# Two matmul bursts of a recurrent group in halves, with the last level's sums between, on one Trainium2 core

## The reference, cut to what matters

```python
def step(s, rkvw):
    r_t, k_t, v_t, w_t = rkvw
    a = k_t[..., :, None] * v_t[..., None, :]
    out = jnp.einsum('bhi,bhij->bhj', r_t, u * a + s)
    s = a + w_t[..., :, None] * s
    return (s, out)
...
_, out = jax.lax.scan(step, s0, rkvw)
```

## Time and profile before

| what | value |
|---|---|
| median of 3 runs | 4139.7 us (4137.18 to 4140.56) |
| the profiled execution, its own time | 4149.18 us |
| its span, first to last instruction | 4147.4 us |
| PE busy | 3717.0 us, 90% |
| VectorE, ScalarE, GpSimd busy | 63%, 52%, 40% |
| mean granted TensorE clock | 0.954 |

### The profile page before, as it was taken

How to read it: one execution, slowest core, us unless ns; L and a number is a source line. 1 busy time by engine, 2 the same in 40 slices (tenths; PEclk the granted TensorE clock), 3 DMA queues, 4 the chain that set the end, 5 groups by cost and what they waited for, 6 DMA issues and landing times. The chain is left out here.

```text
span 4147.4 us, 66284 instructions
## 1 busy us (share of the span) xinstructions
PE 3717.0 (90%) x24448; PEld 2274.3 (55%) x24448; DVE 2623.6 (63%) x5691; ACT 2149.6 (52%) x4272; POOL 1650.5 (40%) x1849
## 2 busy tenths in 40 slices
PE   7988899898898889999988888998998889899898
PEld 4544575645554457464655445656465454565556
DVE  4765736766676573676667657467666765646766
ACT  5755743433675574343466657334347575733434
POOL 3554443222455445322245444422325544542232
PEclk9999999999998999999999999999999999999999
DMA  4032220202303222020320412211022032221102
GB/s 137 17 95 71 82 81 26 77 11 78 110 16 96 70 82 81 22 81 11 110 77 15 120 54 83 72 40 63 22 102 80 29 106 56 77 71 42 61 25 109
DMA packets 94528, 275.81 MB, mean 67 GB/s; under 512 B 25472, under 2 KB 25984, under 8 KB 73088
## 3 DMA queue, kind: packets, MB, share of 16 engines
q1 hardware_dynamic: 94208, 271.58, 20.4%
HBM read 201.24 MB, written 4.19 MB: 50 GB/s over the span
## 5 line engine op out<-in xcount | busy, mean ns | idle before, releaser
L813 POOL TENSOR_SCALAR probs<-probs,row_inv 128x512 f32<-128x512 f32 x1024 | 693.0, 692 | 643.6 <-DVE row_inv L728 643.5
L672 ACT ACTIVATE probs<-probs,row_max 128x512 f32<-128x512 f32 x1024 | 733.6, 726 | 129.4 <-DVE row_max L744 128.3
L567 PE MATMUL ps<-ident,probs 128*128 128x128 f32 x4096 | 608.9, 290 | 173.4 <-ACT pT L666 147.2
L567 PEld LDWEIGHTS ps<-ident,probs 128*128 128x128 f32 x4096 | 478.8, 147 | 383.7 <-ACT pT L666 210.7
L666 ACT ACTIVATE pT<-ps 128x512 f32<-128x512 f32 x768 | 430.5, 602 | 113.0 <-PE ps L567 112.3
L377 PE MATMUL ps<-mix,wring 128*128 128x512 f32 x1024 | 477.5, 603 | 5.0 <-DMA wring<-in_blocks_dram 3.4
L542 PE MATMUL ps<-kstack,qstack 96*128 96x512 f32 (+1 forms) x1024 | 380.2, 466 | 19.0 <-DVE row_max L744 10.4
L744 DVE CUSTOM_DVE_ANT_0 probs<-ps,maskA 128x512 f32<-128x512 f32 x512 | 329.3, 681 | 43.9 <-PE ps L542 43.9
L744 DVE CUSTOM_DVE_ANT_0 probs<-ps,neg 128x512 f32<-128x512 f32 x512 | 340.6, 685 | 8.8
L377 PEld LDWEIGHTS ps<-mix,wring 128*128 128x128 f32 x1024 | 193.9, 192 | 204.2 <-issue 184.8
L1543 POOL TENSOR_TENSOR hinv<-hvar,minus_half 128x32 f32<-128x32 f32 x24 | 146.2, 6093 | 378.8 <-DVE hvar L1263 378.8
(11 more groups left out here) (178 smaller groups left out, 7022.5 us busy)
## 6 DMA issues: line engine op xcount, KB each, us to landing
wring<-in_blocks_dram SPq DMA_DIRECT2D x151, 1024.0 KB, 5.2
qstack<-hi SPq DMA_DIRECT2D x256, 64.0 KB, 2.0
kstack<-hi SPq DMA_DIRECT2D x256, 64.0 KB, 2.0
maskA<-in_mask_dram SPq DMA_DIRECT2D x9, 1024.0 KB, 7.6
rows<-in_rows_dram SPq DMA_DIRECT2D x8, 1024.0 KB, 5.9
qstack<-hi SPq DMA_DIRECT2D x256, 32.0 KB, 2.0
qstack<-lo SPq DMA_DIRECT2D x128, 64.0 KB, 2.0
kstack<-lo SPq DMA_DIRECT2D x128, 64.0 KB, 2.0
```

Of the source, the lines that this page charges most:

```text
L567: ins = nc.tensor.transpose(tile[:, qc * P:(qc + 1) * P], probs[:, m % PSLOTS, qc, kc * P:(kc + 1) * P], ident[:, :])
L672: nc.scalar.activation(p, p, ACT.Exp, bias=row_max[:, n % PSLOTS, qc:qc + 1], scale=-1.0, accum_out=row_sum[:, n % PSLOTS, qc:qc + 1]).the ...
L813: nc.gpsimd.tensor_scalar(p, p, row_inv[:, (n - 1) % PSLOTS, qc:qc + 1], 1.0, ALU.mult, ALU.mult)\
```

## The change

In the recurrent groups:

- `fresh_state` and `from_state` take a list of token tiles. Each burst is run as two halves, tiles (0, 1) and (2, 3). The semaphore updates stay at the last tile, the waits at the first.
- `pair_sums4` takes a part. Part 0 stands between the halves of `fresh_state`, part 1 behind them.
- `bonus_high` takes a part. Part 0 stands ahead of `from_state`, part 1 between its halves.
- On VectorE `bonus` level 4 becomes `bonus4(hg, part)`. Part 0 stays where it was; part 1 moves behind `states` and `spread`. `states` is divided into `new_states` (line 1233's joins) and `states` (the scans), with nothing between them.

```diff
-            def pair_sums4(hg):
+            def pair_sums4(hg, part):
                 pe.wait_ge(*dve_done.when('rk', l, hg, 4))
-                for part in range(2):
-                    nc.tensor.matmul(take(pe, 'sums4', l, hg, part), head_sum[:, :], rk4[:, 2 * part:2 * part + 2, :, :],
-                                     start=True, stop=True).then_inc(*tile_ready.reach('sums4', l, hg, part))
+                nc.tensor.matmul(take(pe, 'sums4', l, hg, part), head_sum[:, :], rk4[:, 2 * part:2 * part + 2, :, :],
+                                 start=True, stop=True).then_inc(*tile_ready.reach('sums4', l, hg, part))
...
-            def bonus_high(hg):
+            def bonus_high(hg, part):
                 by8 = y_bank.rearrange('p (b two t) -> p b two t', two=2, t=4)
-                for s in range(4):
-                    if s % 2 == 0:
-                        pe.wait_ge(*dve_emptied.when('sums4', l, hg, s // 2))
+                pe.wait_ge(*dve_emptied.when('sums4', l, hg, part))
+                for s in (2 * part, 2 * part + 1):
                     m = nc.tensor.matmul(by8[:, :, 1, :], centre[:, :], rk4[:, s, :, :], start=False, stop=False,
                                          skip_group_check=True)
-                m.then_inc(*S['context_ready'].reach('high', l, hg))
+                m.then_inc(*S['context_ready'].reach('high', l, hg, part))
...
-                fresh_state(hg)
-                pair_sums4(hg)
+                fresh_state(hg, (0, 1))
+                pair_sums4(hg, 0)
+                fresh_state(hg, (2, 3))
+                pair_sums4(hg, 1)
                 bonus_low(hg)
                 middle(hg, 1)
                 if hg == C - 1:
                     gate(C - 1)
                 if hg > 0:
                     roots_to_features(hg - 1)
-                bonus_high(hg)
-                from_state(hg)
+                bonus_high(hg, 0)
+                from_state(hg, (0, 1))
+                bonus_high(hg, 1)
+                from_state(hg, (2, 3))
                 middle(hg, 2)
...
                 if hg > 0:
-                    dve.wait_ge(*S['context_ready'].when('high', l, hg - 1))
+                    dve.wait_ge(*S['context_ready'].when('high', l, hg - 1, 1))
...
-                bonus(hg, 4)
+                bonus4(hg, 0)
+                new_states(hg)
                 states(hg)
                 spread(hg)
+                bonus4(hg, 1)
                 if hg > 0:
                     normalise(hg - 1)
```

More of the change, by code:

```diff
@@ L962, in keys_to_tokens, with fresh_state @@
                 m.then_inc(*tile_ready.reach('kt', l, hg))
[L964 to L969, removed]
+            def fresh_state(hg, tiles):
+                if 0 in tiles:
+                    for level in range(3):
+                        pe.wait_ge(*dve_emptied.when('sums', l, hg, level))
+                    pe.wait_ge(*act_emptied.when('vt', l, hg))
+                    pe.wait_ge(*act_emptied.when('kt', l, hg))
+                for tc in tiles:
                     for r in range(4):
@@ L976, in fresh_state, with from_state @@
                                                  start=True, stop=True)
[L977 to L986, removed]
+                if C - 1 in tiles:
+                    m.then_inc(*S['fresh_ready'].reach(l, hg))
+            def from_state(hg, tiles):
+                if 0 in tiles:
+                    pe.wait_ge(*dve_done.when('r8', l, hg))
+                    pe.wait_ge(*dve_done.when('fresh', l, hg))
+                    pe.wait_ge(*act_done.when('other', l, hg))
+                    pe.wait_ge(*act_done.when('pairs', l, hg))
+                    pe.wait_ge(*dve_done.when('pairs', l, hg))
+                for tc in tiles:
                     for p in range(4):
@@ L1209, in bonus @@
                 dve.wait_ge(*act_emptied.when('vp', l, hg))
[L1210 to L1227, removed]
@@ L1229, in states @@
-            def states(hg):
+                dve.wait_ge(*tile_ready.when('sums', l, hg, level))
+                if level == 0:
+                    out, i0, i1 = rk0[:, :], ps[:, 0, :], v
+                elif level == 1:
+                    out, i0, i1 = rk1[:, :], ps[:, 1, 0:256], tokens(v, 1)[:, :, 0, 0]
+                else:
+                    out, i0 = rk2[:, :, :, :], ps[:, 2, :].rearrange('p (s b t) -> p s b t', s=2, t=2)
+                    i1 = tokens(v, 2)[:, :, 0, :].rearrange('p b s -> p s b').unsqueeze(3).to_broadcast([P, 2, L // 4, 2])
@@ new lines, in bonus @@
+                nc.vector.tensor_tensor(out, i0, i1, ALU.mult).then_inc(*dve_emptied.reach('sums', l, hg, level))
+            def bonus4(hg, part):
+                dve.wait_ge(*tile_ready.when('sums4', l, hg, part))
+                two = slice(2 * part, 2 * part + 2)
+                i0 = ps[:, ring.bank('sums4', l, hg, part), :].rearrange('p (s b t) -> p s b t', s=2, t=4)
+                i1 = tokens(vT[:, hg % 2, :], 4)[:, :, 0, two].rearrange('p b s -> p s b').unsqueeze(3)\
+                    .to_broadcast([P, 2, L // 8, 4])
+                nc.vector.tensor_tensor(rk4[:, two, :, :], i0, i1, ALU.mult)\
+                    .then_inc(*dve_emptied.reach('sums4', l, hg, part))
@@ L1230, in states, with new_states @@
+            def new_states(hg):
                 dve.wait_ge(*act_done.when('other', l, hg))
@@ L1236, in states @@
                 ins.then_inc(*dve_done.reach('fresh', l, hg))
+            def states(hg):
                 dve.wait_ge(*dve_done.when('fresh', l, hg))
```

3 lines of the change are left out of this document (2 added, 1 removed).

## The result

The changed kernel takes 4167.12 us (median of 6 runs, 4160.81 to 4174.76) against 4136.43 us for the kernel before on the same chip (6 runs, 4122.88 to 4140.56): a ratio of 1.0073, 95% interval 1.0056 to 1.0089. It is slower by 30.7 us. The forecast was +7.4 us; the range to 4170 us held the time, but the likeliest bin, no measurable difference, was wrong.

The account below looks back on a forecast made before the run. PE's own instruction list plus its waits was taken to bound each group. 21.6 us (ordinary groups) + 9.8 (last groups) - 24 (relief) = +7.4 us, the profiled execution going from 4149.2 to 4156.6, median 4147; range 4132 to 4170.

Parts of the forecast that it names:

- likeliest bin: Whole kernel: time within about 0.2% (8.3 us) of the kernel before; chance 0.43.
- The halves: Split bursts on PE: each half takes 0.95 us to the next line; splitting `fresh_state` costs PE 0.28 us.
- The state chain: From `fresh_state` to `from_state`: joins start at about 4.21 us, `pairs` comes 0.24 us earlier, `from_state` can start at 11.38.
- The structure: Added time in the recurrent groups: 21.6 us over 24 ordinary groups plus 9.8 us over 8 last groups.
- The relief: Gaps and low clock around the bursts: 24 us of some 39 go away; bounds 0 and 39.
- more than nine: Test in the new profile: more than nine stretched halves would show the prediction wrong.
- under 8 us of "issue" waits: Test in the new profile: PE's "issue" waits at the bursts fall from about 15 us to under 8.
- forecast gap: PE's stop in a stretched burst: a gap of 2.1 us, start to start, shrinks to 0.9 to 1.
- No relief: Rival on the bursts' gaps and low clock: none of it goes; +31 us, up to +40, 4171 to 4180; chance 0.2.
- Full relief: Rival on the bursts: no gaps or low clock remain; -8 to -12 us, 4128 to 4132; chance 0.15.
- switches cost nothing: Rival on PE's weight-load switches: they hide under running matmuls; 22 us, with relief -2 (4138); chance 0.1.
- the change does nothing: Rival at `from_state`: the wait still covers part 1 of `bonus_high`; within 3 us of 4140; chance 0.07.

Follow-up runs that it names:

- e10: Changed kernel with `spread` (ScalarE's half of `pairs`) moved ahead of the copy of rT on ScalarE; 4159.29 us, ratio 1.0044 to the kernel before.
- e4_again: The kernel before, unchanged, profiled once more; 4119.88 us in one run.
- e6: Kernel before with one token tile of `fresh_state` issued twice in one early group, 64 more PE records; 4135.80 us, ratio 0.9978.
- e7: Kernel before with two token tiles of `fresh_state` issued twice in one early group, 128 more PE records; 4151.05 us, ratio 1.0025.
- e8: Kernel before with three token tiles of `fresh_state` issued twice in one early group, 192 more PE records; 4136.96 us, ratio 0.9990.
- e11: Kernel before with `spread` (ScalarE's half of `pairs`) moved ahead of the copy of rT on ScalarE; 4136.90 us, ratio 1.0004.
- e9: Changed kernel with 128 more PE records issued once in its first group; 4180.73 us, ratio 1.0094 to the kernel before.
- e1: Kernel before with only `fresh_state` in halves, `from_state` whole and VectorE's order as before; 4138.80 us, ratio 0.9998.
- e5: Changed kernel with `from_state` whole, behind both parts of `bonus_high`; 4151.95 us, ratio 1.0032 to the kernel before.
- e2: Kernel before with only `from_state` in halves, part 1 of `bonus_high` between, `fresh_state` whole; 4178.66 us, ratio 1.0099.
- e3: Kernel before with only VectorE's order changed, part 1 of `bonus4` behind `spread`, both bursts whole; 4144.64 us, ratio 1.0020.

## Why the prediction was wrong in size

**Right in kind.** PE's list is what bounds a group; part 1 of `bonus_high` leaves a wait that hid it; PE idles about 0.6 us ahead of `from_state` (0.62); no ring bank and no VectorE part makes PE wait in the changed kernel; gaps shrink rather than grow. The sums between the halves take 1.06 us (688.82 to 689.88) and those behind them 0.97 (690.87 to 691.84), exactly the 0.86 with 0.11 and 0.09 for the switches.

**The halves** take 0.99 us to the next line (687.83 to 688.82), not 0.95. That is 0.08 us more in each of the two bursts: the split of `fresh_state` costs PE 0.36 us (687.83 to 691.84 is 4.01, against 3.65 in the earlier trace rows), not 0.28, and the block of `from_state` grows by 1.22, not 1.14.

**The state chain was the first step that failed.** It was to come 0.24 us earlier in an ordinary group; it came 0.06 later (11.68 against 11.62). The joins did start earlier (4.30 against 4.45, with 4.21 forecast). What took the gain back is in the rows: the joins start 0.09 us later than forecast; the scans last 4.17 us instead of 4.04 in the kernel before (its rows follow); and ScalarE's `pairs` starts 0.09 after VectorE's, held by the copy of rT, which follows PE's later projection. Together that is the 0.30 us missing, within rounding.

```profile
693.16 0.61 POOL L1548 COPY rstd_j<-hinv 128x512 f32<-128x512 f32 x1
693.49 4.04 DVE L1240 TENSOR_TENSOR_SCAN entry<-w,s0c,fresh 128x63 f32<-128x63 f32 x16
```

e10 confirms the last one: without that hold `from_state` comes 0.07 us earlier in a second group and 0.30 in a first. That the scans are longer because GpSimd's copy falls into them is an inference from overlaps (below), not an experiment of its own.

**The structure was therefore mis-sized:** 24 x 0.90 + 8 x 1.23 = 31.4 us was forecast; 8 x (1.37 + 1.29 + 1.29) + 8 x 1.42 = 31.6 + 11.4 = 43.0 came. In an ordinary second group the 1.29 are the 0.90 of the forecast, 0.30 from the chain (11.68 instead of 11.38) and 0.08 from the halves of the block. So the larger part of this error is the chain's.

**The relief was the other half of the error.** 24 us of 39 were to go, and the prediction said itself that no row shows it. By the medians 43.0 - 30.7 = 12.3 us came back, if nothing outside the groups changed. So of the 23.3 us between forecast and result (30.7 - 7.4) 11.6 are structure (43.0 - 31.4) and 11.7 relief (24 - 12.3). Against the one profile that I had read the relief looks larger, 41.8 - 22.9 = 18.9 us, but that profile had more stretch than the next: e4_again has 24.0. The six traces with TensorE's order of before, shifted or not (before, e4, e6, e7, e8, e11), have 34.9 us on average, the three with its order of the change (after, e9, e10) 24.4; the difference of 10.5 is near the 12.3 of the medians. I had taken the stretch of one execution for a property of the kernel, and I had taken it that the gaps would stay as many. The trace after has fourteen groups with over 0.5 us of stretch, against thirteen and eight before; my own test, "more than nine" stretched halves, came out against me. The test of under 8 us of "issue" waits failed too: 7.1 + 3.8 = 10.9 us, down from 15.4. One small slip: the rows put the records from the 64th to the 91st 0.015 us apart (1.43 - 1.02 over 27), not 0.012; it moves the forecast gap by 0.1 us.

Which part brings relief? Stretch alone doesn't settle it: e1 and e5, with `fresh_state` in halves, have 20.5 and 20.2 us, the changed kernel 22.9, and e2, with only `from_state` in halves, 38.4; but each is one execution, and two of the kernel before differ by 17.8 us. The granted clock settles more. In the five traces with `fresh_state` in halves (after, e1, e5, e9, e10) the clock is at 1.2 GHz for 7 to 24 us in all inside the groups; in the eight with it whole (before, e4, e2, e3, e6, e7, e8, e11) for 27 to 48 us, and no figure of one kind reaches into the other. The gaps at the edges add up to 8.7 to 15.6 us in the first five and 8.0 to 19.2 in the other eight, which overlap. On average it is 17.1 us at low clock against 38.8, at half speed worth some 11 us (an estimate), and 11.2 us of gaps against 13.9. So the relief comes from the first burst, and in the main through less time at low clock; in the two profiles read here it went from 47.8 to 17.1 us. Why the clock fell less often no experiment took apart.

The low clock costs time without any gap too. A last group of the changed kernel, on PE's timeline, and the window from its burst (line 973's busy us and records of PE and PEld, granted clock, DMA):

```profile
743.64 1.12 PE L973 MATMUL ps<-v_blocks,k_tok 32*32 32x128 f32 x64
744.69 2.08 PE L931 MATMUL ps<-rk,head_sum 128*128 128x512 f32 x2
746.69 1.44 PE L973 MATMUL ps<-v_blocks,k_tok 32*32 32x128 f32 x64
...
743.64:749.20 5.56, 2.56 (x128) 1.68 (x128) 0.69 0.03 6
```

Here the sums take 2.08 us instead of 1.12, and the second half 1.44 instead of 1.07, with no idle time named. Up to line 938 (749.02) this is 5.38 us instead of 4.01. The clock fell to 1.2 GHz 0.9 us after the burst's start, after a wait of 0.69 us and `variance`; the packet's edge comes only at 747.62, so this is not a hidden gap. In this group 1.46 us are lost (16.58 against 15.12), as much as in the last groups of the kernel before with low clock and no gap (1.5).

**The rivals.** *No relief* (4171 to 4180, chance 0.2) was nearest in time, but for the wrong reason: its +31 was structure alone with nothing given back; in fact the structure was 43.0 and about 12 was given back. That it matches the measured +30.7 is luck. *Full relief*, *switches cost nothing* and *the change does nothing* are refuted by 22.9 us of stretch, by the 0.20 us of switches in either burst, and by 27.50 us a group.

**The fastest version tried** is e6_shift64, at 0.9978: a shift of the packets by a few matmuls issued twice, not an improvement of the work. e8_shift192 can't be told from no change, and e7 is slower. It would not survive another edit of the program.

## What to carry to other kernels

- Before a burst is split to let something start earlier, ask what stood in the shadow of the wait in front of it. Here a matmul group of 0.86 us that was free became 0.86 us of the path, in each of 32 groups, and an experiment with that part alone (e2) was 40.1 us slower.
- A chain's earlier start is worth only what its last link delivers: check each engine's order near its end (another copy ahead, a neighbour's work in parallel), and expect two late arrivals that are nearly tied to hide each other.
- Gaps and low clock found in one profile are not a budget: profile the same kernel twice first. Here two executions of one kernel differed by 17.8 us in stretch, over twice the forecast effect.

## What the runs showed of the hardware that was not expected

**Scans are slowed by a GpSimd copy beside them.** Sixteen scans of 128x63 took 3.96 us with no copy of `rstd_j` in parallel (a first group of the changed kernel, below), 4.04 in the kernel before with an overlap of 0.3 us, 4.17 where the copy overlaps them by about 0.4 us (693.83 to 694.24, above), and 4.32 where all of it lies inside, in e3; there the copy also takes 0.76 us instead of 0.61.

```profile
666.33 3.96 DVE L1248 TENSOR_TENSOR_SCAN entry<-w,s0c,fresh 128x63 f32<-128x63 f32 x16
```

The more they overlap, the longer the scans. The Trainium skill's page "SBUF — State Buffer", section "Who interferes with whom", says that a VectorE instruction with two SBUF inputs contends with a GpSimd instruction that reads SBUF. The rows agree in that both engines lose time (4.32 and 0.76 us in e3). The page calls the contention an exclusive lock; whether a whole scan is blocked the rows don't show, and no run here moved the copy alone.

**Where PE stops is only partly a property of the program.** The same program gave thirteen stretched groups in one execution and eight in another, seven of them the same in both, and every stop at a packet's edge; shifts of a quarter, a half and three quarters of a packet moved the places and changed the median by -0.22%, +0.25% and -0.10% (the last not told from zero). What decides between two executions of one kernel stays open.
